# Graph layers on one Trainium2 core: edges sorted by both end nodes, end rows picked by TensorE instead of gathered

## What is computed

```python
fs = (x @ Ws + bs).reshape(-1, H, D)
fd = (x @ Wd + bd).reshape(-1, H, D)
e = jax.nn.leaky_relu(fs[src] + fd[dst], 0.2)
logits = jnp.einsum('ehd,hd->eh', e, attn)
m = jax.ops.segment_max(logits, dst, num_segments=N)
ex = jnp.exp(logits - m[dst])
denom = jax.ops.segment_sum(ex, dst, num_segments=N)
alpha = ex / denom[dst]
out = jax.ops.segment_sum(alpha[:, :, None] * fs[src], dst, num_segments=N)
```

## Time and profile before

| | us |
|---|---|
| median of three runs | 3487.92 |
| profiled execution: span from first to last instruction | 3439.5 |
| what lies around the span, if the profiled execution took the median | 48.4 |
| sorting stage up to the sorted edges | 159.7 |
| from there to the first sums of target rows | 12.9 |
| first pass, 161 tiles | 494.1 |
| from its end to the first softmax row | 16.4 |
| second pass, 161 tiles | 427.0 |
| from its end to the first softmax row | 27.6 |

### The profile page before, as it was taken

How to read it: one execution, slowest core, us unless ns; L and a number is a source line. 1 busy time by engine, 2 the same in 40 slices (tenths; PEclk the granted TensorE clock), 3 DMA queues, 4 the chain that set the end, 5 groups by cost and what they waited for, 6 DMA issues and landing times.

```text
span 3439.5 us, 38430 instructions
## 1 busy us (share of the span) xinstructions
PE 2715.4 (79%) x11874; PEld 1940.1 (56%) x11874; DVE 2169.9 (63%) x5194; ACT 1354.2 (39%) x2276; POOL 722.0 (21%) x756
## 2 busy tenths in 40 slices
PE   6877777586866765678999999967875888787998
PEld 3422222284423322467989989936643454666998
DVE  7788888894444443679877768857645325765332
ACT  5855555460233322156655556606412110533110
POOL 2056666400477773200000000020000000000000
PEclk9999999897988887689999999978986979896999
DMA  9745555432465662077655656540000011001220
GB/s 304 251 137 144 144 144 138 132 95 101 125 157 161 164 151 70 20 256 257 239 203 202 213 194 212 194 147 1 14 12 32 7 36 69 1 14 56 83 83 22
DMA packets 95207, 428.64 MB, mean 125 GB/s; under 512 B 27061, under 2 KB 27317, under 8 KB 89812
## 3 DMA queue, kind: packets, MB, share of 16 engines
q1 hardware_dynamic: 49690, 263.43, 23.3%
q0 software_dynamic: 45296, 162.38, 16.6%
HBM read 375.28 MB, written 50.44 MB: 124 GB/s over the span
## 4 chain that ended last, share of the span: by engine, by line
PE 57%; DVE 16%; issue 11%; ACT 6%; POOL 6%; DMA 4%; SPq 0%; ACTq 0%; DVEq 0%; POOLq 0%
PE PS L849 11%; PE PS L1094 7%; PE PS L991 6%; PE PS L896 5%; PE PS L799 4%; POOL WB L663 3%; PE PS L993 3%; PE PS L796 3%; DVE W L1769 2%; POOL logits L676 2%; ACT PS L1234 2%; PE PS L882 2%; PE PS L1012 1%; DVE w1s L2043 1%; DMA WB<-src_rows,idx 1%
## 5 line engine op out<-in xcount | busy, mean ns | idle before, releaser
L991 PE MATMUL PS<-urowsT,w1s 128*128 128x384 f32 (+2 forms) x1164 | 366.5, 378 | 55.7 <-issue 30.8
L849 PE MATMUL PS<-WB,XT 128*125 128x384 f32 (+1 forms) x1120 | 383.5, 504 | 23.0 <-DMA WB<-in_L_gnn_Wos 12.5
L817 PE MATMUL PS<-O,WB 125*128 x644 | 288.7, 588 | 139.7 <-ACT PS L1251 124.1
L663 POOL DMA_INDIRECT WB<-src_rows,idx x322 | 311.8, 968 | 308.0 <-DVE idf L1601 113.1
L676 POOL DMA_INDIRECT logits<-lgr,key x322 | 318.8, 990 | 224.4 <-DVE lgr L1688 138.3
L849 PEld LDWEIGHTS PS<-WB,XT 128*125 128x125 f32 x1120 | 212.2, 191 | 186.9 <-issue 34.0
L993 PE MATMUL PS<-urowsT,w1s 128*128 128x192 f32 (+2 forms) x1164 | 303.3, 261 | 0.0
L896 PE MATMUL PS<-F,PT 125*125 125x96 f32 (+3 forms) x1500 | 288.9, 345 | 18.2 <-ACT PT L1285 8.2
L817 PEld LDWEIGHTS PS<-O,WB 125*128 125x128 f32 x644 | 131.5, 223 | 296.8 <-issue 262.9
L1721 DVE SCALAR_TENSOR_TENSOR WB<-PS,WB 128x776 f32<-128x776 f32 x161 | 155.7, 967 | 227.0 <-PE PS L817 226.4
L1251 ACT COPY PS<-WB 128x776 f32<-128x776 f32 x161 | 130.3, 809 | 393.5 <-DMA WB<-src_rows,idx 289.6
(11 more groups left out here) (342 smaller groups left out, 5284.4 us busy)
## 6 DMA issues: line engine op xcount, KB each, us to landing
XN<-in_L_ffn_w SPq DMA_DIRECT2D x98, 769.0 KB, 4.3
PB<-in_L_ffn_w SPq DMA_DIRECT2D x97, 768.0 KB, 5.4
logits<-NEG SPq DMA_DIRECT2D x8, 1367.2 KB
WB<-logits SPq DMA_DIRECT2D x5, 2187.5 KB
WB<-targets SPq DMA_DIRECT2D x20, 512.0 KB, 4.5
slot_rows<-NEG POOLq DMA_DIRECT2D x13, 768.0 KB, 62.3
slot_outs<-NEG POOLq DMA_DIRECT2D x12, 768.0 KB, 91.7
C<-in_L_ffn_expert_w SPq DMA_DIRECT2D x8, 1152.0 KB, 5.4
```

The lines of the kernel that those rows point to most:

```text
L663: pool.indirect_dma_start(out=gs[u], out_offset=None, in_=src_rows, in_offset=bass.IndirectOffsetOnAxis(ap=source[:, i:i + 1], axis=0)).th ...
L817: mm = pe.matmul(zw[i % 4][:, half, :], ohT[i % 2], O[0:R, bass.ds(c, 1), half * (GW // 2):(half + 1) * (GW // 2)] .rearrange("p o n -> p ...
L849: mm = pe.matmul(PS[0:R, 4 + g % 4, 0:hw], XT[:, k, t * R:(t + 1) * R], w[:, k, half * hw:(half + 1) * hw], start=(k == 0), stop=(k == kc ...
L991: pe.matmul(both(q % 2, columns), w1s[:, g % 2, 0, w:w + P], urowsT2[:, :, k * TU:k * TU + columns], start=k == 0, stop=False)
```

## The change

The edges are sorted into 25 buckets, target block by source block, so that both rows of an edge come from one known block of 125. Every bucket is padded to whole tiles, and the list gets 181 tiles. Both tables stay in SBUF as two parts in the rounded fp32 format, which PE reads in one go: the large part is the table rounded by ACT, the small part the difference, made by DVE in place. PE picks and adds both rows by one-hots, a large and a small part each, so four matmuls stand where one full fp32 matmul stood (which the trace shows as two). Gone are the store of the source table, the gathers, and ACT's copies into PSUM. Counting takes one matmul of 128 columns. The one-hots for it and for the places move to POOL; ACT makes the one-hots of both ends (256 columns). Logits are finished and scattered in groups of four tiles. The norm runs ahead of the ranking, and DVE's scan replaces doubling steps.

```diff
-CH = 16
-HA = 392
-ES = (E + T * (P - 1)) // P
+CH = 8
+NQ = T * T
+ES = (E + NQ * (P - 1)) // P
+EW = -(-ES // 4) * 4
+HB = D // 2
...
-            in_two(lambda a, b: X[a:b], lambda a, b: ins["x"].rearrange("(t p) d -> p t d", p=R)[a:b], s_x)
...
-                for t in range(T):
-                    sp.wait_ge(s_frow, T * 2 * g + t + 1)
-                    in_two(lambda a, b: src_rows[t * R + a:t * R + b, :], lambda a, b: F[a:b, t, 0:GW], s_tab)
...
+            def place_onehots():
+
+                pool.wait_ge(s_place, 1)
+                for t in range(ET):
+                    wait(pool, s_pm, t - NB + 1)
+                    pool.tensor_scalar(ohq[t % NB], iota16, place_in[:, t:t + 1], None, ALU.is_equal).then_inc(s_q, 1)
+
+            def count_onehots(i):
+                wait(pool, s_ohu, i - 7)
+                pool.tensor_scalar(oht[i % 8], iota16, idf[:, 1, i:i + 1], None, ALU.is_equal)
+                pool.tensor_scalar(ohs[i % 8], iota16, idf[:, 0, i:i + 1], None, ALU.is_equal).then_inc(s_oh, 1)
...
-                pool.wait_ge(s_lg, ES * g + i + 1)
+                if i % 4 == 0:
+                    pool.wait_ge(s_lg, -(-ES // 4) * g + i // 4 + 1)
...
-                for i in range(ES + LAG):
-                    if i < ES:
-                        gathers(i)
...
+                for i in range(ES):
+                    if g == 0 and i + LAG < ES:
+                        count_onehots(i + LAG)
+                    scatter(i, g)
...
+            def block(i, side):
+                return pe.value_load(blocks[0:1, side, i:i + 1], min_val=0, max_val=T - 1)
+
+            def node_rows(out, i, cd, cs, a, b, first=True):
+
+                for side, c in ((0, cs), (1, cd)):
+                    for part in (large, little):
+                        mm = pe.matmul(out, ohT[i % 3][:, (1 - side) * P:(2 - side) * P],
+                                       part[side][:, bass.ds(c, 1), a:b].rearrange("p o n -> p (o n)"),
+                                       start=first, stop=side == 1 and part is little, skip_group_check=True)
+                        first = False
+                return mm
...
                 for i in range(ES):
-                    wait(pe, s_wa, i)
+                    cs, cd = now
+                    wait(pe, s_zr, i)
                     pe.wait_ge(s_oh, i + 1)
...
+                    pe.matmul(tallied[:, bass.ds((cd * T + cs) * P, P)], oht[i % 8], ohs[i % 8], start=False,
+                              stop=i == ES - 1, skip_group_check=True).then_inc(s_ohu, 1)
                     pe.wait_ge(s_tt, i + 1)
...
+                    node_rows(zA, i, cd, cs, 512, GW, first=False).then_inc(s_za, 1)
+                    wait(pe, s_mul, i)
+                    node_rows(zB, i, cd, cs, 0, 512).then_inc(s_zp, 1)
+                    now, then = then, (block(i + 2, 0), block(i + 2, 1)) if i + 2 < ES else None
...
                 for i in range(ES):
+                    cs, cd = now
                     pe.wait_ge(s_tt, ES + i + 1)
...
+                    if i >= 4:
+                        pe.wait_ge(s_hd, ES + i - 3)
+                    node_rows(zw[i % 4][:, 0, 0:HB], i, cd, cs, 0, HB)
+                    node_rows(zw[i % 4][:, 1, 0:GW - HB], i, cd, cs, HB, GW).then_inc(s_zp, 1)
+                    now, then = then, (block(i + 2, 0), block(i + 2, 1)) if i + 2 < ES else None
...
+                    act.copy(large[side][:, t, :], (F, O)[side][0:R, t, 0:GW]).then_inc(s_hi, 1)
...
+                    act.activation(tgap[i % 2][0:R], spread_ids[q % 2][0:R, i % CH * 2 * P:(i % CH + 1) * 2 * P],
+                                   ACT.Abs, bias=node[0:R], scale=-1.0).then_inc(s_tg, 1)
...
+                    act.activation(ohT[i % 3], tgap[i % 2][0:R], ACT.Relu, bias=ones[0:R, 0:1],
+                                   scale=-1.0).then_inc(s_tt, 1)
...
+                    act.copy(tails[:, i % EU, :], tail).then_inc(s_tc, 1)
+                    if i + 2 < ES:
+                        turned_gap(i + 2)
+                    if g == 0 and i + 1 < ES:
+                        act.wait_ge(s_wa, i + 1)
+                        act.copy(zA, NEG[:, 0, 0:GW - 512]).then_inc(s_zr, 1)
+                    if i + 2 < ES:
+                        turned_onehot(i + 2)
...
+                link(dve.tensor_tensor(member, bucket.rearrange("p (b t) -> p b t", b=1).to_broadcast([P, NQ, ET]),
...
+                link(dve.tensor_tensor_scan(running.rearrange("p b t -> p (b t)"), ones[:, 0:1].to_broadcast([P, NQ * ET]),
...
+                for b in range(NQ):
+                    ins = dve.scalar_tensor_tensor(out=spread[:, b], in0=running[:, b], scalar=lead[:, b:b + 1],
+                                                   in1=member[:, b], op0=ALU.add, op1=ALU.mult)
                 link(ins)
                 link(dve.tensor_reduce(place_in, spread.rearrange("p b t -> p t b"), AX_X, ALU.add))
...
+                dve.tensor_tensor(little[side][:, t, 0:GW], (F, O)[side][0:R, t, 0:GW], large[side][:, t, :].bitcast(F32),
+                                  ALU.subtract).then_inc(s_lo, 1)
...
+            def whole_rows(g):
+
+                dve.wait_ge(s_zp, ES * (g + 1))
+                for t in range(T):
+                    dve.tensor_tensor(rows(t, F), little[0][:, t, 0:D].bitcast(F32), large[0][:, t, 0:D].bitcast(F32),
+                                      ALU.add).then_inc(s_whole, 1)
...
+                for i in range(ES):
+                    weigh_end(i)
+                    if i:
+                        head_sums(i - 1)
+                    weigh_start(i)
+                    if i % 4 == 0 and i:
+                        finish(0, i - 1)
...
-            dve.wait_ge(s_idx, 48)
-            rank_edges()
             dve.wait_ge(s_x, 32)
             layer_norm(0, X, XN, tr=0)
+            dve.wait_ge(s_idx, 48)
+            rank_buckets()
```

More of the change, by code:

```diff
@@ L244, in build @@
+        spread = Oz[:, 0:NQ * ET].rearrange("p (b t) -> p b t", b=NQ)
+        block_of = Fz[:, 2048:2048 + 2 * ET].rearrange("p (k t) -> p k t", k=2)
+        bucket = Fz[:, 2370:2370 + ET]
+        in_bucket, tiles_in, upto, until, lead, ends = [Fz[:, 2700 + 32 * k:2700 + 32 * k + NQ] for k in range(6)]
         tile_of, place_in, src1, dst1 = [F[:, k, GW:GW + ET] for k in range(4)]
-        qgap = [F[:, k, GW + 160:GW + 224].bitcast(F16) for k in range(2)]
         ohq = [(O if b < 15 else F)[:, b % 15 // 3 if b < 15 else 4, GW + 64 * (b % 3):GW + 64 * (b % 3) + 64].bitcast(F16)
@@ L294, in build @@
         PSz = PS[:, :, :].rearrange("p b n -> p (b n)")
[L295 to L298, removed]
+        zw = [PS[:, 2 * b:2 * b + 2, :] for b in range(4)]
+        zA = PS[:, 6, P:P + GW - 512]
+        zB = PS[:, 7, 0:512]
+        tallied = PSz[:, 0:NQ * P]
         s_const = sem("consts_loaded")
@@ L1543, in rank_edges @@
-                dve.tensor_copy(tally[:, 0, 0:T], old[:, :, ET - 1]).then_inc(s_rowt, 1)
-                units, end, start, base = [tally[:, k, 0:T] for k in range(1, 5)]
-                dve.wait_ge(s_roff, 1)
-                link(dve.tensor_scalar(units, PS[:, 7, 8:8 + T], 63.5, 1.0 / P, ALU.add, ALU.mult))
-                link(dve.tensor_scalar(units, units, ROUND, None, ALU.add))
-                link(dve.tensor_scalar(units, units, ROUND, None, ALU.subtract))
-                link(dve.tensor_copy(end[:, 0:1], units[:, 0:1]))
@@ L1571, in rank_edges @@
                 dve.wait_ge(s_place, 1)
-                link(dve.tensor_scalar(chunkf, tile_at[:, 0:ES], end[:, 0:1], None, ALU.is_ge))
-                for b in range(1, T - 1):
-                    link(dve.scalar_tensor_tensor(out=chunkf, in0=tile_at[:, 0:ES], scalar=end[:, b:b + 1], in1=chunkf,
-                                                  op0=ALU.is_ge, op1=ALU.add))
-                link(dve.tensor_copy(chunk, chunkf))
             def edge_values(a, b):
@@ new lines, in whole_rows, with finish @@
+            def whole_rows(g):
[3 more added lines that the diff above has]
+                                      ALU.add).then_inc(s_whole, 1)
+            def finish(g, i):
+                a, n = i // 4 * 4 % EU, i % 4 + 1
+                h = HEADS[g]["h"]
+                dve.wait_ge(s_hd, ES * g + i + 1)
+                for k in range(4):
+                    last = i // 4 * 4 + k - EU
+                    if last >= 0 and k < n:
+                        dve.wait_ge((s_alt if g else s_sc)[k], 16 * (last // 4 + 1))
+                dve.scalar_tensor_tensor(out=lgr[:, a:a + n, 0:h], in0=dots[:, a:a + n, 0:h], scalar=0.8,
+                                         in1=tails[:, a:a + n, 0:h], op0=ALU.mult, op1=ALU.add).then_inc(s_lg, 1)
```

491 lines of the change are left out of this document (218 added, 273 removed).

## The result

Five runs of the changed kernel took 3503.11 to 3512.57 us, median 3504.32; the kernel before took 3488.56 beside them. The ratio is 1.0049 with a 95% interval of 1.0033 to 1.0065: **slower by about half a per cent**. The forecast was 3493, with 3468 to 3538 as its range and slower as the likeliest sign. So range and sign held. The terms inside did not: sort and both passes were costed too low, and the base was wrong by 47 us the other way.

What follows compares the result with a forecast made beforehand. PE's instruction sequencer was taken to bound both passes and DVE the sort. Terms 19.6 - 21.7 + 4.9 + 7 - 5 = +4.8 us made a span of 3444, plus 48.4 around it 3493; range 3468 to 3538.

Steps and rivals of the forecast that it cites:

- the base: Whole kernel before: profiled span 3439.5 us plus 48.4 us around it, kept unchanged, tied to the median of 3487.92.
- POOL's 2.56 us: Second pass before: a gather of 0.97 and a scatter of 0.99, 0.30 idle before each, 2.56 us a tile.
- The step: Second pass: PE's sequencer paces each tile at 2.39 us, 181 tiles making 433, the stage 434 or 435, +7 us.
- the eight address steps: Both passes, each tile: eight matmuls with register-addressed operands take a sequencer step of 0.125 us each, 1.00 in all.
- the sequencer's floor: First pass: loads 1.30, count matmul 0.14, eight matmuls' address steps 1.00 and a wait 0.1 make 2.54 us a tile.
- I take 2.60: First pass: 2.60 us taken as a tile's pace, giving 472.4 us against 494.1, -21.7 us.
- the two-tile loop: First pass: PE writes the second bank for the next tile only after weighing ends at 2.95 us; fits by under 0.1.
- at 0.4 they stay under DVE's pace: Sort: POOL's 157 place one-hots at 0.4 us each stay under DVE's pace of about 0.7 us a tile.
- The tails: After each pass: the first pass's tail goes from 16.4 to 21.3 us, +4.9; the second pass's changes by -5.
- POOL's one-hots as the bound of the first pass: Rival, chance 0.18: above 0.66 us a one-hot POOL paces the first pass; at 0.76, +38 us, 3531.
- PE's sequencer doesn't bind: Rival, chance 0.13: loads and address steps cost nothing; second pass 292 us, first 400, whole kernel 3278.
- The clock: Rival, chance 0.07: second pass at PE's lower clock, 1.2 GHz, needs 2.6 us a tile, up to +45 us, 3538.

## Why the prediction was right or wrong

The forecast's stages, those of three profiles before and of two after, in us (the list's end is left out, the first sums of rows stand for the sort and the link):

| | before, three profiles | forecast | after, two profiles |
|---|---|---|---|
| first sums at | 172.6, 172.0, 172.9 | 192.2 | 200.7, 201.4 |
| first pass | 494.1, 496.3, 499.6 | 472.4 | 497.1, 497.3 |
| its tail | 16.4, 16.7, 16.3 | 21.3 | 20.4, 20.9 |
| attention and linear layers | 211.7, 212.6, 212.7 | 211.7 | 211.7, 211.7 |
| second pass | 427.0, 468.2, 476.7 | 434 | 450.7, 451.1 |
| its tail | 27.6, 27.0, 27.0 | 22.6 | 24.4, 24.8 |
| the rest | 2090.1, 2090.9, 2092.6 | 2090.1 | 2103.0, 2098.6 |
| around the span | 1.8 | 48.4 | 1.8 |

**The base failed.** "With the 48.4 us around it, which I keep" was wrong: 1.8 us lie around a span. The other 47 lay inside the stages, 41 to 50 us of it in the second pass, whose first profile was the quick one of three. So the forecast's reading that POOL's 2.56 us paces that pass fits the quick execution, 2.65 a tile, and not the other two, 2.91 and 2.96. A difference of span and median is no stretch around the span until a run with its own span shows it.

**Second pass, mechanism right, size short.** The step was 2.39 us a tile; it was 2.48 on average. The loads took 1.31, as said; the eight address steps 1.08 for 1.00. 181 x 0.09 is 16 us. Against a usual execution of before the stage isn't 7 us slower but 17 to 26 faster, because in such an execution POOL waited some 40 us longer, for a reason that stays open.

**First pass, the sequencer's floor named but undersized, 25 us short.** The term "I take 2.60" fell in two ways. The sequencer's floor isn't 2.54 but 2.72: two loads 1.33 for 1.30, the count matmul 0.21 for 0.14, eight steps 1.07 for 1.00. And with that the two-tile loop, which I had put just above the floor, isn't reached; a pace that fits it appears at 2.33, once the check and POOL are out of the way. No wait for ACT or DVE shows in the pace.

**Sort, right owner, one term missing.** DVE is the bound and ACT idle, as said. The list (its last cast ends at 191.0) came 13 us after the forecast's 178.0. The missing term is in "at 0.4 they stay under DVE's pace": POOL's one-hots do stay under it, and still cost DVE 12 us, 116 starts by 0.105. The other terms together came out some 2.5 us shorter, which of them was not worked out, and two operations of 3925 columns add 3.4:

```profile
L1556 DVE TENSOR_TENSOR_SCAN F<-ones,WB 128x3925 bf16<-128x3925 f32 x1 | 8.3, 8327 | 0.0
...
L1582 DVE TENSOR_REDUCE F<-O 128x157 f32<-128x3925 f32 x1 | 7.1, 7068 | 0.0
```

The scan took 8.3 us where the bounds were 4.2 and 7.6, the sum 7.1 where 6 was taken. The Trainium skill, "DVE: opcode table, instruction layouts, handler registers and perf-mode slots", section "6. Datapath and trigger behaviour", says that the built-in scan runs at half throughput; the trace agrees, 8.3 us being twice the 4.2 that the forecast took as the lower bound. The way from the list to the first sums took 9.7 us instead of 14.2, which gave 4.5 back.

On POOL beside DVE, the Trainium skill, "SBUF — State Buffer", section "Who interferes with whom", says that a one-input operation of DVE in a fast mode and any operation of GpSimd exclude each other, the later one waiting for the whole of the first. The trace agrees that they are in each other's way and not on how far: a DVE one-hot loses about 0.105 us to a POOL one-hot of 0.60, not the whole of it. Whether DVE's one-hots run in such a mode no run here shows.

**The tails** were right: 20.4 for 21.3, 24.4 for 22.6.

**The rest** took 2093 to 2104 us in the seven profiles with the change's passes that compute everything, and 2090 to 2093 in the three of before, with the same number of matmuls. The longest three have a granted clock of 0.88 instead of 0.89 over the stretch. The seven are 8 us longer on average; whether the clock makes that difference, and why it is granted less, stays open.

**The sum**: 8.5 + 25 - 1 + 17 + 2 + 13 - 47 makes 17 us over the forecast for the profiled run (3509.7 us). Errors of some 66 us upwards and 48 downwards made a good number: that it lies in the range is luck.

**Where the loss is.** Against the second profile of before, a more usual execution, the changed one is 24 us longer: the first sums come 29 us later and the rest takes 12 more, the tails and the linear layers come out even, the second pass gives 17 back, and the first pass, held by the sequencer, gives nothing.

**Signs.** Of what the prediction said would show it, the loads at 0.65 and the weight loads idle for "issue" came, and so did DVE's 90% in the sort. Its sign of being wrong, a sort that ends after 190 us, came by a hair (190.7), the array was busy 72% of the second pass and not at most 60%, and both passes were longer than said.

**Rivals.** POOL's one-hots as the bound of the first pass: they measured 0.63 and 0.60 us against a point of 0.66, so it missed by little, and with the check gone it came true. By the rule cited there, which is for two inputs where a one-hot has one, and taken at its worst, a one-hot was 0.5; the trace makes it 0.60, 2.4 times DVE's 0.25. PE's sequencer doesn't bind: refuted by the kernel without the check. The clock: granted 0.94 over the second pass, so it cost single tiles, not the stage.

## What to carry to other kernels

When the engines of a stage are all idle part of the time and the array's idle time says "issue", add up the sequencer's own instructions: a register loaded with a range check cost 0.65 us here, without it 0.36, and two checks a tile, over both passes, were worth 143 us, where the whole change lost 16. Work moved to POOL isn't free because POOL has time: see what DVE does beside it. And before stages are compared, profile the kernel before more than once; the stage with a gather and a scatter in each tile moved by 50 us between three profiles, every other one by under 6.

## What the runs showed of the hardware

Not expected were four things. A sequencer load of two numbers takes 0.52 us, of one 0.30 (0.58 and 0.36 to the next instruction). Of DVE's 314 one-hots of 184 columns 116 lost 0.10 us each while POOL made its 128-column ones. A POOL one-hot of 128 columns takes 0.60 to 0.64 us. And a pass with a scatter of 128 rows each tile, four in flight, didn't get under 336 us for 181 tiles, 1.86 each, though half of them followed within 1.47.
